# The evacuation copies of the second layer's transposed attention weights go from ScalarE to VectorE

## The chip, the cores and the metric

The kernel runs as one program on the eight cores of a Trainium2 chip. Each core takes one of the eight sequences of the batch (2048 tokens of 1024 values) through two transformer layers; the cores exchange nothing. The metric is the device time of the slowest core, in microseconds (us), from one launch. Of the engines of a core, four matter here: PE (TensorE, the matrix engine, with PEld for its weight loads), DVE (VectorE), ACT (ScalarE) and POOL (GpSimd, which issues most DMAs).

## The reference, cut to what matters

Two layers. Each normalizes x, computes attention and a mixture-of-experts feed-forward part from the normalized input, and adds both to x. Only the attention of the second layer is touched by the change:

```python
def _L1_attn_ref(x, Wq, bq, Wk, bk, Wv, bv, proj):      # 16 heads of 64
    q = jnp.einsum('bse,hde->bhsd', x, Wq) + bq[None, :, None, :]
    k = jnp.einsum('bse,hde->bhsd', x, Wk) + bk[None, :, None, :]
    v = jnp.einsum('bse,hde->bhsd', x, Wv) + bv[None, :, None, :]
    causal = jnp.triu(jnp.ones((s, s), bool), 1)
    scores = jnp.einsum('bhsd,bhtd->bhst', q, k) / scale  # scale = 8
    scores = jnp.where(causal[None, None], -jnp.inf, scores)
    att = jax.nn.softmax(scores, axis=-1) / scale
    z = jnp.einsum('bhst,bhtd->bhsd', att, v).reshape(b, s, h * dh)
    return z @ proj
```

## The kernel before, in words

The program runs stage by stage: for layer 0 the normalization with routing, the experts, q/k/v, statistics and attention, then the same for layer 1 without the statistics. Attention of layer 1 (`attn1_pass`, from line 931) is the last stage before the output is stored. x stays in SBUF all the time (`x_tm`).

`attn1_pass` walks over 16 blocks of 128 query rows (`qt` 0 to 15). Block `qt` sees `Lq = (qt+1)*128` keys because of the causal mask, so the work of a block grows from 128 to 2048 keys. This text counts blocks from 1: block 1 has 128 keys, block 16 has 2048. Inside a block the 16 heads go through a software pipeline: at step `i`, the scores of head `i` (`st_scores`), the softmax of head `i-1` (`st_soft`), and the transposes of head `i-2` (`st_pt`) are written out; after each odd head its pair's product with v (`st_ctx`) follows. A step whose transposed head is even is called an A step below (its tiles are `pbufA`, `ptbA`), the other a B step (`pbufB`, `ptbB`, then `st_ctx`).

The parts of a step, with their lines:

- Scores: PE multiplies q and k into four PSUM banks of 512 columns (`psA`, L950). DVE copies the even tiles to SBUF (`sc_sb`, L963 or L976), ACT the odd ones (L966 or L979), and DVE adds the mask to the last 128 columns (L969).
- Softmax: DVE takes the row maximum (L987) and scales it (L991), ACT computes the exponentials with their sum (L995, `pbuf`), and DVE then does three things with them: it scales the sum (L1001), takes the reciprocal (L1005), and multiplies the whole row of `pbuf` by it (L1008).
- Transposes: PE transposes `pbuf` of head `i-2` in pieces of 128 columns into PSUM (`ptp`, bf16, L1021). Each parity of head has one half of `ptp`, room for eight pieces. After eight pieces, or after the last one, they are copied to SBUF as `ptb` (L1028). In blocks 1 to 8 a head has one such copy, in blocks 9 to 16 two: the first of 1024 columns, and the second of the rest. The second group of transposes writes the same half of `ptp`, so it waits for the first copy.
- Product with v: PE multiplies v and `ptb` of both heads of the pair into `psB` (L1041); ACT copies the result out (L1051).

After each second block the output projection (L1078) is added to x (L1087).

What sets the order: every engine works through its own list in the order in which the Python code writes the operations (`Prog.op`); nothing reorders them. `flush` gives semaphores to dependencies between engines. A wait at the head of an engine's list therefore holds everything behind it on that engine, but nothing on another engine that doesn't depend on it.

Of the kernel before, what the change touches and what calls it, by code (L numbers as in the profile page):

```python
# [315 lines left out]
def build_program(T=2048, taps=(), stop_after=None):  # L316
# [19 lines left out]
    with ctx:  # L336
        p = Prog(nc, ctx)
# [593 lines left out]
        def attn1_pass(ph, q_fm, k_fm, v_tm):  # L931
# [82 lines left out]
            def st_pt(qt, h):  # L1014
                hb = h % 2
                pb = pbufA if hb == 0 else pbufB
                ptb = ptbA if hb == 0 else ptbB
                seg = []
                for kc in range(qt + 1):
                    slot = hb * 8 + kc % 8  # L1020
                    p.op("tensor", lambda e, kc=kc, slot=slot, pb=pb: e.transpose(  # L1021
                            ptp[:, slot * 128:(slot + 1) * 128],
                            pb[:, kc * 128:(kc + 1) * 128], id_b[:]),
                         r=[(pb, kc), (id_b, None)], w=[(ptp, hb)])
                    seg.append(kc)
                    if len(seg) == 8 or kc == qt:
                        k0 = seg[0]
                        p.op("scalar", lambda e, k0=k0, kc=kc, hb=hb, ptb=ptb: e.copy(  # L1028
                                ptb[:, k0 * 128:(kc + 1) * 128],
                                ptp[:, hb * 1024 + (k0 % 8) * 128:  # L1030
                                    hb * 1024 + (k0 % 8) * 128 + (kc + 1 - k0) * 128]),
                             r=[(ptp, hb)],
                             w=[(ptb, k) for k in seg])
                        seg = []
# [23 lines left out]
            for qt in range(NCH):  # L1058
                Lq = (qt + 1) * 128
                ntile = (Lq + 511) // 512  # L1060
                for i in range(16 + 3):
                    if i < 16:
                        st_scores(qt, i, Lq, ntile)
                    if 0 <= i - 1 < 16:
                        st_soft(qt, i - 1, Lq, ntile)
                    if 0 <= i - 2 < 16:
                        st_pt(qt, i - 2)
                        if (i - 2) % 2 == 1:
                            st_ctx(qt, i - 2)
# [219 lines left out]
```

How the kernel before makes its waits and increments, by code:

```python
    def wait_all_dma(self, eng, sem_name):  # L172
        s = self.dma_sems[sem_name]
        h, v = s[0], s[1]
        self.op(eng, lambda e: e.wait_ge(h, v))
# [29 lines left out]
                def body(e, entries=entries):  # L205
                    for ent in entries:
                        for (s, v) in ent.waits:
                            e.wait_ge(s, v)
                        inst = ent.fn(e)
                        for (s, k) in ent.incs:
                            inst.then_inc(s, k)
```

## Time and profile before

| | |
|---|---|
| median of 3 runs | 7202.99 us (7201.66 to 7204.07) |
| the profiled execution's own time | 7199.1 us |
| its span, core 3 (the slowest) | 7197.5 us |
| spans of the eight cores | 7181.2 to 7197.5 us |
| busy: PE / DVE / ACT | 4996.4 / 2258.2 / 1461.7 us |
| attention of layer 1, core 3 | from about 5303 to 7174 us |
| PE / DVE / ACT busy in it | 825.4 / 836.5 / 776.0 us of 1871 |

A timeline row of the profile gives the start, the duration, the engine, the line, the operation with its tiles, and in brackets how long the engine sat idle before it and what released it. Busy shares of the whole span are averages over stages with different limits: the experts' stages keep PE busy nearly all the time, while in the attention of layer 1 no engine is busy for even half of it.

### The profile page before, as it was taken

The numbers are of one execution on the slowest core, as the hardware profiler recorded it, in microseconds if no ns is written. First come the engines' busy times: TensorE is split into PE (matmuls) and PEld (weight loads), VectorE is DVE, ScalarE is ACT, GpSimd is POOL, SyncE is SP. The second block draws the span as 40 slices with busy tenths as digits, with TensorE's granted clock in tenths as the row PEclk, the third lists the DMA queues.
The fourth block names the chain that finished last, engine by engine and source line by source line (L and its number), as shares of the span: only waits on it lengthen the run. The fifth ranks groups of instructions, "written<-read, shape, count | busy, mean of one in ns | idle before, by whom it ended". The sixth has DMA issues, their size and how long they took to land. (4 is left out here: it accounts for less than half of the span.)

```text
span 7197.5 us, 67809 instructions; the slowest of 8 cores (7181.2 to 7197.5 us)
## 1 busy us (share of the span) xinstructions
PE 4996.4 (69%) x23786; PEld 2350.9 (33%) x23786; DVE 2258.2 (31%) x4515; ACT 1461.7 (20%) x2461; POOL 174.0 (2%) x318
## 2 busy tenths in 40 slices
PE   2399998673444427999999999999864444444443
PEld 2244443321111223444444444444331222222222
DVE  3333343321223232222222222222234444444443
ACT  2211110001112221101100011101013344434443
POOL 0000000000000000000000000000000000000000
PEclk9999999755666558999999999999975555555555
DMA  1122211003222102212222122220101000000001
GB/s 48 28 37 36 36 24 30 7 15 47 38 35 33 21 0 49 45 28 37 49 37 40 21 49 49 37 40 9 30 15 18 12 12 1 12 12 1 12 1 56
DMA packets 70700, 199.15 MB, mean 28 GB/s; under 512 B 8025, under 2 KB 28762, under 8 KB 60512
## 3 DMA queue, kind: packets, MB, share of 16 engines
q0 software_dynamic: 63136, 177.79, 14.9%
q1 hardware_dynamic: 7232, 17.02, 0.7%
q8 instruction: 198, 3.24, 0.2%
q14 instruction: 134, 1.10, 0.1%
HBM read 364.17 MB, written 8.39 MB: 52 GB/s over the span
## 5 line engine op out<-in xcount | busy, mean ns | idle before, releaser
L1141 PE MATMUL p_gps<-s_xn_fm,s_wgr 128*128 128x512 bf16 x4672 | 1773.4, 380 | 32.8 <-DMA s_wgr<-wg 32.8
L1149 PE MATMUL p_gps<-s_xn_fm,s_wur 128*128 128x512 bf16 x4672 | 1773.2, 380 | 12.2 <-DMA s_wur<-wu 12.2
L1167 PE MATMUL p_yps<-s_wd_sb,s_hfm 128*128 128x512 bf16 x4672 | 1011.6, 379 | 0.2 <-DVE s_x_tm L1175 0.2
L1160 DVE TENSOR_TENSOR s_hfm<-p_gps,s_sil 128x512 bf16<-128x512 f32 x584 | 403.8, 691 | 1656.4 <-ACT s_sil L1158 1656.4
L1158 ACT ACTIVATE s_sil<-p_gps 128x512 f32<-128x512 f32 x584 | 348.7, 597 | 2565.1 <-PE p_gps L1141 2508.7
L1141 PEld LDWEIGHTS p_gps<-s_xn_fm,s_wgr 128*128 128x128 bf16 x4672 | 457.6, 98 | 585.3 <-issue 35.4
L1149 PEld LDWEIGHTS p_gps<-s_xn_fm,s_wur 128*128 128x128 bf16 x4672 | 457.6, 98 | 565.8 <-issue 16.2
L1167 PEld LDWEIGHTS p_yps<-s_wd_sb,s_hfm 128*128 128x128 bf16 x4672 | 452.7, 98 | 556.0 <-issue 33.9
L1175 DVE SCALAR_TENSOR_TENSOR s_x_tm<-p_yps,s_cw_tm,s_x_tm 128x1024 f32<-128x1024 f32 x256 | 328.6, 1284 | 499.7 <-PE p_yps L1167 499.6
L1021 PE MATMUL p_ptp<-s_id_b,s_pbufB 128*128 128x128 bf16 x1088 | 147.9, 306 | 430.8 <-ACT s_ptbB L1028 271.8
L1021 PE MATMUL p_ptp<-s_id_b,s_pbufA 128*128 128x128 bf16 x1088 | 148.3, 306 | 341.3 <-ACT s_ptbA L1028 282.2
L987 DVE TENSOR_REDUCE s_sm_sc<-s_sc_sb 128x1 f32<-128x128 f32 (+15 forms) x256 | 326.5, 1276 | 0.1
L511 PE MATMUL p_xtp<-s_id_f,s_xnrot 128*128 128x128 f32 x256 | 62.1, 423 | 349.6 <-DVE s_xnrot L507 349.6
L950 PE MATMUL p_psA<-s_k_fm,s_q_fm 64*128 64x512 bf16 (+3 forms) x640 | 274.4, 554 | 22.5 <-DVE s_sc_sb L969 8.7
L918 PE MATMUL p_psA<-s_woring,s_cfm 128*128 128x512 bf16 x256 | 121.1, 585 | 233.7 <-DMA s_woring<-woT 212.9
L761 PE MATMUL p_pq<-s_xn_fm,s_wring 128*128 128x512 bf16 x1024 | 244.4, 383 | 52.3 <-DVE s_q_fm L771 19.7
L976 DVE COPY s_sc_sb<-p_psA 128x512 f32<-128x512 f32 x256 | 176.1, 690 | 303.8 <-PE p_psA L950 303.8
L1021 PEld LDWEIGHTS p_ptp<-s_id_b,s_pbufB 128*128 128x128 bf16 x1088 | 102.6, 136 | 514.6 <-issue 514.6
L1041 PE MATMUL p_psB<-s_ptbB,s_v_tm 128*64 128x128 bf16 x1088 | 138.9, 310 | 166.9 <-ACT s_ptbB L1028 166.9
L1021 PEld LDWEIGHTS p_ptp<-s_id_b,s_pbufA 128*128 128x128 bf16 x1088 | 101.6, 136 | 423.6 <-issue 423.6
L995 ACT ACTIVATE s_pbufA<-s_sc_sb,s_sm_sc 128x128 bf16<-128x128 f32 (+15 forms) x128 | 153.7, 1201 | 332.1 <-DVE s_sm_sc L991 332.1
L995 ACT ACTIVATE s_pbufB<-s_sc_sb,s_sm_sc 128x128 bf16<-128x128 f32 (+15 forms) x128 | 153.7, 1201 | 240.8 <-DVE s_sm_sc L991 240.3
(191 smaller groups left out, 4039.7 us busy)
## 6 DMA issues: line engine op xcount, KB each, us to landing
s_woring<-woT POOLq DMA_DIRECT2D x128, 256.0 KB, 4.4
s_wgr<-wg POOLq DMA_DIRECT2D x29, 1024.0 KB, 16.7
s_wur<-wu POOLq DMA_DIRECT2D x29, 1024.0 KB, 21.6
s_wd_sb<-wd POOLq DMA_DIRECT2D x10, 2816.0 KB, 20.8
s_prring<-proj POOLq DMA_DIRECT2D x64, 256.0 KB, 4.2
s_wd_sb<-wd POOLq DMA_DIRECT2D x9, 1024.0 KB, 10.0
s_x_tm<-x SPq DMA_DIRECT2D x1, 8192.0 KB, 32.0
out<-s_x_tm SPq DMA_DIRECT2D x1, 8192.0 KB, 22.5
```

Of the source, the lines that this page charges most:

```text
L761: p.op("tensor", lambda e, dc=dc, ts=ts, slot=slot, oc_l=oc_l: e.matmul(pq[:, (ts % 4) * 512:(ts % 4) * 512 + TS], wring[:, slot * 2048 + ...
L950: p.op("tensor", lambda e, oc=oc, prt=prt, qt=qt, j0=j0, w512=w512, bk=bk: e.matmul(psA[:, bk * 512:bk * 512 + w512], q_fm[prt:prt + 64, o ...
L976: e.tensor_copy(sc_sb[:, hb * T + j0:hb * T + j0 + w512], psA[:, bk * 512:bk * 512 + w512])
L987: p.op("vector", lambda e, Lq=Lq, hb=hb: e.reduce_max(sm_sc[:, hb * 4:hb * 4 + 1], sc_sb[:, hb * T:hb * T + Lq], axis=AX.X, negate=True), ...
L995: p.op("scalar", lambda e, pb=pb, Lq=Lq, hb=hb, qt=qt: e.activation(pb[:, 0:Lq], sc_sb[:, hb * T:hb * T + Lq], AF.Exp, bias=sm_sc[:, hb * ...
L1021: p.op("tensor", lambda e, kc=kc, slot=slot, pb=pb: e.transpose(ptp[:, slot * 128:(slot + 1) * 128], pb[:, kc * 128:(kc + 1) * 128], id_b[:]),
L1141: p.op("tensor", lambda e, dc=dc, ts=ts, lo=lo, rslot=rslot, gp=gp: e.matmul(gp, wgr[:, rslot * 4096 + dc * 512 + lo: rslot * 4096 + dc * ...
L1149: p.op("tensor", lambda e, dc=dc, ts=ts, lo=lo, rslot=rslot, up=up: e.matmul(up, wur[:, rslot * 4096 + dc * 512 + lo: rslot * 4096 + dc * ...
L1158: p.op("scalar", lambda e, ssl=ssl, gp=gp, gb=gb: e.activation(ssl, gp, AF.Silu), r=[(gps, ("g", gb))], w=[(sil, gb)])
L1160: p.op("vector", lambda e, fc=fc, ts=ts, ssl=ssl, up=up, gb=gb: e.tensor_tensor(hfm[:, fc * T + ts * TSL:fc * T + (ts + 1) * TSL], up, ssl ...
L1167: p.op("tensor", lambda e, fc=fc, half=half, c=c, yb=yb: e.matmul(yps[:, yb * 1024 + half * 512:yb * 1024 + (half + 1) * 512], hfm[:, fc * ...
L1175: p.op("vector", lambda e, c=c, yb=yb, e_=e_: e.scalar_tensor_tensor(x_tm[:, c * D:(c + 1) * D], yps[:, yb * 1024:(yb + 1) * 1024], cw_tm[ ...
```

## The change

One line. The copy of the transposed weights from PSUM to SBUF (L1028) is issued on the VectorE instead of the ScalarE, with the same operands; it has the same place in the code, in `st_pt`, behind the softmax of the head before.

```diff
@@ -1025,7 +1025,7 @@
                     seg.append(kc)
                     if len(seg) == 8 or kc == qt:
                         k0 = seg[0]
-                        p.op("scalar", lambda e, k0=k0, kc=kc, hb=hb, ptb=ptb: e.copy(
+                        p.op("vector", lambda e, k0=k0, kc=kc, hb=hb, ptb=ptb: e.tensor_copy(
                                 ptb[:, k0 * 128:(kc + 1) * 128],
                                 ptp[:, hb * 1024 + (k0 % 8) * 128:
                                     hb * 1024 + (k0 % 8) * 128 + (kc + 1 - k0) * 128]),
```

The lists of PE, POOL and SP stay as they are. Two places show what moves. First the DVE's list in block 4 (512 keys), before; each step is one softmax with the score copies of the next head behind it (`s_pbufA`/`s_pbufB` are the weights, `s_sc_sb` the scores, `p_psA` their PSUM banks):

```order
L1008 TENSOR_SCALAR s_pbufA<-s_pbufA,s_sm_sc 128x512
L963 COPY s_sc_sb<-p_psA 128x384
L969 TENSOR_TENSOR s_sc_sb<-p_psA,s_causal 128x128
L987 TENSOR_REDUCE s_sm_sc<-s_sc_sb 128x1
L991 TENSOR_SCALAR s_sm_sc<-s_sm_sc 128x1
L1001 TENSOR_SCALAR s_sm_sc<-s_sm_sc 128x1
L1005 RECIPROCAL s_sm_sc<-s_sm_sc 128x1
L1008 TENSOR_SCALAR s_pbufB<-s_pbufB,s_sm_sc 128x512
```

The same place on DVE after the change:

```order
L1008 TENSOR_SCALAR s_pbufA<-s_pbufA,s_sm_sc 128x512
L1028 COPY s_ptbB<-p_ptp 128x512
L963 COPY s_sc_sb<-p_psA 128x384
L969 TENSOR_TENSOR s_sc_sb<-p_psA,s_causal 128x128
L987 TENSOR_REDUCE s_sm_sc<-s_sc_sb 128x1
L991 TENSOR_SCALAR s_sm_sc<-s_sm_sc 128x1
L1001 TENSOR_SCALAR s_sm_sc<-s_sm_sc 128x1
L1005 RECIPROCAL s_sm_sc<-s_sm_sc 128x1
L1008 TENSOR_SCALAR s_pbufB<-s_pbufB,s_sm_sc 128x512
L1028 COPY s_ptbA<-p_ptp 128x512
```

The copy of the other parity's head now stands between the multiplication of L1008 and the next score copy. On ACT in block 16 (2048 keys), this stood before, with the copy behind the exponential of L995:

```order
L966 COPY s_sc_sb<-p_psA 128x384
L995 ACTIVATE s_pbufB,s_sm_sc<-s_sc_sb,s_sm_sc 128x2048
L1028 COPY s_ptbA<-p_ptp 128x1024 x2
L979 COPY s_sc_sb<-p_psA 128x512
L966 COPY s_sc_sb<-p_psA 128x384
L995 ACTIVATE s_pbufA,s_sm_sc<-s_sc_sb,s_sm_sc 128x2048
L1028 COPY s_ptbB<-p_ptp 128x1024 x2
L1051 CAST s_zfm<-p_psB 64x128 x2
```

and on DVE in block 16 this stands after the change:

```order
L987 TENSOR_REDUCE s_sm_sc<-s_sc_sb 128x1
L991 TENSOR_SCALAR s_sm_sc<-s_sm_sc 128x1
L1001 TENSOR_SCALAR s_sm_sc<-s_sm_sc 128x1
L1005 RECIPROCAL s_sm_sc<-s_sm_sc 128x1
L1008 TENSOR_SCALAR s_pbufB<-s_pbufB,s_sm_sc 128x2048
L1028 COPY s_ptbA<-p_ptp 128x1024 x2
L976 COPY s_sc_sb<-p_psA 128x512 x2
L969 TENSOR_TENSOR s_sc_sb<-p_psA,s_causal 128x128
```

Both copies of a head have gone from behind the exponential on ACT to behind L1008 on DVE.

## Rows read from the trace of the kernel before

**Rows 1.** Waits, core 3, 5303 to 7174 us: us in total, times, longest.

```profile
ACT s_pbufA L995 <- DVE s_sm_sc L991: 332.1, 127, 28.9
...
PE p_ptp L1021 <- ACT s_ptbA L1028: 282.2, 64, 5.9
PE p_ptp L1021 <- ACT s_ptbB L1028: 271.8, 64, 5.7
...
DVE s_sm_sc L1001 <- ACT s_pbufB L995: 202.0, 128, 4.1
```

**Rows 2.** Busy time by stretch: us, PE, PEld, DVE, ACT, POOL, granted clock.

```profile
5303.00:5870.00 567.00, 237.55 (x1316) 105.68 (x1315) 267.73 (x840) 213.72 (x527) 12.67 (x24) 0.51 0.08 12
5870.00:7174.00 1304.00, 587.83 (x3930) 314.34 (x3928) 568.73 (x1056) 562.29 (x847) 20.07 (x38) 0.51 0.05 8
```

**Rows 3.** Timeline, an A step of block 16: start, us, engine, line, operation.

```profile
7076.57 0.99 ACT L1028 COPY s_ptbA<-p_ptp 128x1024 bf16<-128x1024 bf16 x1
...
7077.30 0.75 DVE L1008 TENSOR_SCALAR s_pbufB<-s_pbufB,s_sm_sc 128x2048 bf16<-128x2048 bf16 x1
...
7077.70 1.01 PE L1021 MATMUL p_ptp<-s_id_b,s_pbufA 128*128 128x128 bf16 x8 [5.68 <-ACT s_ptbA L1028]
...
7078.65 1.88 PE L950 MATMUL p_psA<-s_k_fm,s_q_fm 64*128 64x512 bf16 x4
7078.81 1.01 ACT L1028 COPY s_ptbA<-p_ptp 128x1024 bf16<-128x1024 bf16 x1 [1.25 <-PE p_ptp L1021]
...
7079.71 1.29 DVE L976 COPY s_sc_sb<-p_psA 128x512 f32<-128x512 f32 x2 [1.66 <-PE p_psA L950]
```

**Rows 4.** Timeline, the B step of block 16 before it, from its second copy.

```profile
7066.20 1.01 ACT L1028 COPY s_ptbB<-p_ptp 128x1024 bf16<-128x1024 bf16 x1 [1.25 <-PE p_ptp L1021]
...
7069.17 1.88 PE L950 MATMUL p_psA<-s_k_fm,s_q_fm 64*128 64x512 bf16 x4
```

**Rows 5.** Timeline of block 4: a B step, then an A step.

```profile
5481.49 0.56 ACT L1028 COPY s_ptbB<-p_ptp 128x512 bf16<-128x512 bf16 x1
...
5482.22 0.35 DVE L1008 TENSOR_SCALAR s_pbufA<-s_pbufA,s_sm_sc 128x512 bf16<-128x512 bf16 x1
...
5482.74 0.61 PE L950 MATMUL p_psA<-s_k_fm,s_q_fm 64*128 64x512 bf16 x1
...
5483.45 0.56 DVE L963 COPY s_sc_sb<-p_psA 128x384 f32<-128x384 f32 x1 [0.88 <-PE p_psA L950]
...
5486.60 0.35 DVE L1008 TENSOR_SCALAR s_pbufB<-s_pbufB,s_sm_sc 128x512 bf16<-128x512 bf16 x1
5486.87 0.55 DVE L963 COPY s_sc_sb<-p_psA 128x384 f32<-128x384 f32 x1
```

**Rows 6.** ACT by line and shape: count | busy us, mean ns | idle before.

```profile
L1028 ACT COPY s_ptbB<-p_ptp 128x1024 bf16<-128x1024 bf16 x80 | 79.6, 996 | 14.0 <-PE p_ptp L1021 13.9
...
L1028 ACT COPY s_ptbB<-p_ptp 128x128 bf16<-128x128 bf16 x16 | 4.1, 256 | 5.2 <-PE p_ptp L1021 5.2
```

**Rows 7.** DVE by line and shape, PSUM sources: count | busy us, mean ns | idle before.

```profile
L516 DVE CAST s_xn_fm<-p_xtp 128x1024 bf16<-128x1024 f32 x32 | 39.2, 1225 | 70.1 <-PE p_xtp L511 70.1
...
L963 DVE COPY s_sc_sb<-p_psA 128x128 f32<-128x128 f32 x32 | 9.2, 289 | 3.5 <-PE p_psA L950 3.5
```

**Rows 8.** DVE by line and shape, SBUF sources.

```profile
L843 DVE TENSOR_SCALAR s_ssc<-s_ssc,s_tthr 128x512 f32<-128x512 f32 x28 | 13.6, 486 | 3.0
...
L1008 DVE TENSOR_SCALAR s_pbufB<-s_pbufB,s_sm_sc 128x1152 bf16<-128x1152 bf16 x8 | 4.2, 520 | 1.2 <-DVE s_sm_sc L1005 0.5
...
L1008 DVE TENSOR_SCALAR s_pbufB<-s_pbufB,s_sm_sc 128x1024 bf16<-128x1024 bf16 x8 | 3.9, 487 | 0.9
...
L1008 DVE TENSOR_SCALAR s_pbufB<-s_pbufB,s_sm_sc 128x128 bf16<-128x128 bf16 x8 | 2.0, 254 | 0.9
...
L843 DVE TENSOR_SCALAR s_ssc<-s_ssc,s_tthr 128x256 f32<-128x256 f32 x4 | 1.4, 353 | 0.4
```

**Rows 9.** Timeline, last B copy of block 7: no exponential stands before it.

```profile
5809.89 0.91 ACT L1028 COPY s_ptbB<-p_ptp 128x896 bf16<-128x896 bf16 x1 [1.35 <-PE p_ptp L1021]
```

## The prediction

> **What bounds the kernel now.** I read the page's busy times first, then the busy times of each stretch, then the waits, and then the timeline of single steps. The experts' stages are not touched, so only the attention of layer 1 counts, 1871 us at the end of the program. There no engine is the bound by its busy time: in the first stretch (blocks 1 to 7 and the start of block 8) DVE is busy for 268 of 567 us, in the second for 569 of 1304, and no engine has more than 47% in either [rows 2]. The granted clock is 0.51 in both, the lower of its two levels (1.2 GHz), so a slower stage has no clock left to lose. The stage is a chain of hand-overs. The waits show it: PE waits 554 us for the copies of L1028 (282.2 and 271.8), ACT waits 332 us for DVE before the exponentials of one parity, and DVE waits 202 us for the exponentials of one parity [rows 1].
>
> The timeline shows how a step closes. In an A step of block 16 the first L1028 copy starts on ACT the moment the exponential is done (7076.57) and ends at 7077.56. PE starts the second group of transposes 0.14 us later, the next scores come behind them at 7078.65, and DVE, idle for 1.66 us, starts the next score copies at 7079.71 [rows 3]. Those feed the next maximum and the next exponential. So both the exponential and the copy behind it are on the loop. In a B step PE also waits for the second copy (7066.20 to 7067.21) before the product with v, and the next scores come only behind that product, at 7069.17 [rows 4]. In block 4 a B step closes in the same way: copy at 5481.49, product, scores at 5482.74, DVE idle 0.88 us until 5483.45. An A step there has no such wait: the score copy starts at 5486.87, before L1008 has formally ended at 5486.95, so DVE itself closes the step [rows 5].
>
> **The price of the moved copy.** The change takes 384 copies off ACT (for each of 16 heads one in each of blocks 1 to 8 and two in each of blocks 9 to 16) and puts them on DVE. On ACT they cost 0.256 us for 128 columns and 0.996 for 1024 [rows 6]. A DVE copy of bf16 from PSUM stands nowhere in the trace. From above it is bounded by f32 from PSUM, 0.289 us for 128 columns and 1.225 for 1024, which is 1.045 ns per column [rows 7]. From below it is bounded by bf16 from SBUF, 0.254 and 0.487 us, 0.26 ns per column [rows 8]. In SBUF, f32 costs (486 - 353) / 256 = 0.52 ns per column [rows 8], so there 2-byte values go through at twice the rate of 4-byte ones. I take the PSUM row and halve its rate in the same way, keeping its fixed part (289 - 134 = 155 ns): 0.155 + 0.52 per 1000 columns, so 0.222 us for 128 columns, 0.69 for 1024. That is an estimate from these rows; both ends stay in the range.
>
> The Trainium skill bears on it, in "VectorE: DVE Perf Modes", section "Why PSUM operands drop a tier": a PSUM source rules out the mode that uses both read ports, but leaves the one that packs two 16-bit values per read. The table in "The TRN2 errata" of the same page would give (120 + 512) / 0.96 GHz = 0.66 us for 1024 columns, an estimate by that page, and a sum about 5 us below mine. But the same page of the Trainium skill, under "Mode 1× (REGULAR) — the baseline", names PSUM operands among the cases that the unpacked mode is there for. By that, the time would be that of the slow copy among the rivals. No row here decides between them.
>
> **What the place costs.** The expensive part is where the copy stands, not how long it takes. On ACT it starts when the exponential ends. On DVE it stands behind L1001, L1005 and L1008, all three of which wait for the same exponential. L1008 starts 0.73 us after the point where the ACT copy started, in block 4 (5482.22 - 5481.49) and in block 16 (7077.30 - 7076.57) alike [rows 3, 5]. So the copy starts later by 0.73 us plus L1008's own time, less the 0.08 us by which the next DVE instruction starts before it ends [rows 5]. L1008 lasts 0.25 us in block 1, 0.49 in block 8, 0.52 in block 9 [rows 8] and 0.75 in block 16 [rows 3].
>
> - B step, blocks 1 to 8: later by 0.73 + L1008 - 0.08, and the copy itself is shorter (0.22 for 0.26, 0.69 for 0.99). Block 1: 0.73 + 0.25 - 0.08 - 0.03 = 0.87. Block 8: 0.73 + 0.49 - 0.08 - 0.30 = 0.84. Mean 0.86, all on the loop, because PE does the product and then the next scores, for which DVE waits.
> - A step, blocks 1 to 8: DVE closes the step, so the copy is simply added to it: 0.22 - 0.08 = 0.14 up to 0.69 - 0.08 = 0.61, mean 0.38. On ACT it was hidden: nothing waited for it in such a step, as the product comes a step later.
> - A step, blocks 9 to 16: the first copy (1024 columns) ends later by 0.73 + 0.52 - 0.08 - 0.30 = 0.87 in block 9 and 1.10 in block 16, mean 0.99. The second copy is hidden: in block 16 it can start 1.25 us after the first one ended and would be done at 1.94, while the next scores are ready for DVE only at 2.15 (7079.71 - 7077.56) [rows 3].
> - B step, blocks 9 to 16: the same 0.99, less what the second copy saves (0.03 for 128 columns, 0.32 for 1024 against the 1.01 of [rows 4]), 0.17 in the mean: 0.82.
> - The last B copies of each block have no exponential ahead of them on ACT [rows 9], and on DVE L1008 had to come before the transposes anyway. They only get cheaper: by 0.17 in blocks 1 to 8, by 0.30 + 0.17 = 0.47 in blocks 9 to 16. In blocks 1 to 8 the last A copy is off the path too.
>
> A block has 8 A and 8 B steps. Blocks 1 to 8: 8 x (7 x 0.86 + 7 x 0.38 - 0.17) = 8 x 8.51 = 68. Blocks 9 to 16: 8 x (7 x 0.82 + 8 x 0.99 - 0.47) = 8 x 13.19 = 106. The sum is +174 us. ACT is relieved of 384 copies, which buys nothing: before the exponentials it waits for DVE's L991 in any case [rows 1]. The profiled execution took 7199.1 us, so the sum is 7199 + 174 = 7373; the median of the runs lies 4 us above the profiled one, which makes 7377.
>
> With the copy at its upper bound, blocks 1 to 8 gain another 0.30 per step (mean of 576 columns), and blocks 9 to 16 another 0.54 for the first copy and 0.30 for the second in B steps, in A steps some 0.1 where the second copy would now pass the ready scores (1.25 + 1.225 = 2.48 against 2.15 in block 16, none in block 9). That is 8 x (15 x 0.30) = 36 and 8 x (7 x 0.84 + 8 x 0.64 + 0.84) = 95: +305 us, 7508. With the lower bound each copy is shorter than mine by 0.20 for 1024 columns and by 0.09 in the mean of the others: 8 x 15 x 0.09 = 11 and 8 x (8 x 0.29 + 8 x 0.20) = 31 less: +132 us, 7335.
>
> **Rivals.**
> The slow copy: a bf16 copy from PSUM at the f32 rate. For it: every PSUM row that I have runs at 1.045 ns per column, the one that writes bf16 too [rows 7]. Against it: its sources are all 4-byte. 7508 us.
>
> The delay is absorbed: PE idles more than half of the stage [rows 2], so a later copy might find room and leave the time at 7203. Against it: PE's idle time is the wait for just these copies, and DVE sits idle until the scores behind them are there [rows 3, 5].
>
> The copy escapes the exponential: the copy's data, the transposes, are ready well before, and DVE idles while the exponential runs. If DVE's copy ran in that gap, PE's second transposes and the product would no longer wait for the exponential at all. Counting only the shorter copies (0.17 and 0.47 per head), that gives at least 8 x (16 x 0.17 + 16 x 0.47) = 82 us less, 7121 us. It decides by the order alone: L1028 would have to stand before L1001 on DVE. It stands behind L1008 in every step, so the chance is small.
>
> **How the numbers follow.** The forecast, 7377, has 0.80; the slow copy 0.12; absorbed 0.03; escape 0.03; the last 0.02 is for a loss beyond all of these. The likeliest one's own range is 7335 to 7430. The range for 8 in 10 takes in both bounds of the copy's price: 7330 to 7508. What a measurement of this kernel can tell from no change is about 0.2%, 14 us. Slower holds forecast and slow copy and the rest beyond, 0.94; the same 0.03, faster 0.03.
>
> **What would show it.** After the change, the L1028 rows on DVE should read 0.69 us for 1024 columns and 0.22 for 128, and start 0.08 us before L1008 ends. In block 16 the scores behind an A step start 9.48 us after those behind the B step before it now (7078.65 - 7069.17) [rows 3, 4]; that should become 10.6 us. A pair of steps in block 4 should take 1.2 us more than before. PE's waits for L1028 should name DVE and grow by about 1 us each in blocks 9 to 16. DVE's busy time should grow by about 205 us (384 copies of 0.53 us in the mean), ACT's fall by some 290 (384 of 0.75). The forecast is wrong if the copies start before L1008, if DVE's idle time before L963 and L976 in B steps shrinks by as much as the copy is late, or if the copy's rate is 1.045 ns per column.

## The result, and the profile after

The changed kernel takes 7366.3 us in the median against 7203.6 us of the kernel before, ten runs each; the ratio is 1.0224, with a 95% interval of 1.0212 to 1.0236. It is slower by 163 us. Runs disturbed by a slower state of the chip are left out of this ratio and all that follow, so single medians can differ from it. The profiled execution has a span of 7362.5 us on its slowest core, core 7, 165 us more than before.

The busy times of the page say what moved:

```profile
PE 5003.5 (68%) x23786; PEld 2352.4 (32%) x23786; DVE 2440.8 (33%) x4899; ACT 1194.4 (16%) x2077; POOL 174.0 (2%) x318
```

DVE has 384 instructions and 183 us more than before, ACT 384 fewer and 267 us less. The two engines together do less work and the kernel takes longer: the copies are cheaper on DVE. Their rows, by line and shape (count | busy us, mean ns of one), answer to [rows 6]:

```profile
L1028 DVE COPY s_ptbB<-p_ptp 128x1024 bf16<-128x1024 bf16 x80 | 54.8, 685 | 13.9 <-PE p_ptp L1021 13.9
...
L1028 DVE COPY s_ptbB<-p_ptp 128x512 bf16<-128x512 bf16 x16 | 6.7, 421 | 7.2 <-PE p_ptp L1021 7.2
...
L1028 DVE COPY s_ptbB<-p_ptp 128x128 bf16<-128x128 bf16 x16 | 3.5, 222 | 4.5 <-PE p_ptp L1021 4.5
```

The slope is (685 - 222) / 896 = 0.52 ns per column, half of the f32 rate in [rows 7].

The page's groups of PE show where the time went. Behind the second bar they give how long PE sat idle before the group, and what it waited for. They answer to [rows 1], where PE waited 282.2 and 271.8 us for these copies:

```profile
L1021 PE MATMUL p_ptp<-s_id_b,s_pbufB 128*128 128x128 bf16 x1088 | 148.2, 306 | 483.7 <-DVE s_ptbB L1028 322.9
L1021 PE MATMUL p_ptp<-s_id_b,s_pbufA 128*128 128x128 bf16 x1088 | 149.2, 307 | 402.4 <-DVE s_ptbA L1028 345.7
...
L1041 PE MATMUL p_psB<-s_ptbB,s_v_tm 128*64 128x128 bf16 x1088 | 138.9, 310 | 233.2 <-DVE s_ptbB L1028 231.1
```

PE's waits for the copies in the first two groups grew from 554 to 669 us, by 115 us in 128 waits, 0.9 us each. In the third, the product with v, PE waited 166.9 us for them before and 231.1 now.

The timeline of an A step of block 16 answers to [rows 3, 4]; its first line is where the scores of the B step before it begin (start, us, engine, line, operation, idle before). Before the change, the step of [rows 3] had this line just ahead of its first copy, ACT's read of the exponential's sum:

```profile
7076.48 0.19 ACT L995 ACTIVATION_READ_ACCUMULATOR s_pbufB<-s_sc_sb,s_sm_sc 128x1 f32 x1
```

After it:

```profile
7229.63 1.88 PE L950 MATMUL p_psA<-s_k_fm,s_q_fm 64*128 64x512 bf16 x4
7231.45 1.04 PE L1021 MATMUL p_ptp<-s_id_b,s_pbufA 128*128 128x128 bf16 x8
...
7236.94 0.19 ACT L995 ACTIVATION_READ_ACCUMULATOR s_pbufB<-s_sc_sb,s_sm_sc 128x1 f32 x1
7237.23 0.15 DVE L1001 TENSOR_SCALAR s_sm_sc<-s_sm_sc 128x1 f32<-128x1 f32 x1 [2.30 <-ACT s_pbufB L995]
7237.48 0.16 DVE L1005 RECIPROCAL s_sm_sc<-s_sm_sc 128x1 f32<-128x1 f32 x1
7237.76 0.75 DVE L1008 TENSOR_SCALAR s_pbufB<-s_pbufB,s_sm_sc 128x2048 bf16<-128x2048 bf16 x1
7238.43 0.68 DVE L1028 COPY s_ptbA<-p_ptp 128x1024 bf16<-128x1024 bf16 x1
7239.25 1.01 PE L1021 MATMUL p_ptp<-s_id_b,s_pbufA 128*128 128x128 bf16 x8 [6.77 <-DVE s_ptbA L1028]
7240.20 1.88 PE L950 MATMUL p_psA<-s_k_fm,s_q_fm 64*128 64x512 bf16 x4
7240.37 0.69 DVE L1028 COPY s_ptbA<-p_ptp 128x1024 bf16<-128x1024 bf16 x1 [1.26 <-PE p_ptp L1021]
7240.98 1.47 DVE L976 COPY s_sc_sb<-p_psA 128x512 f32<-128x512 f32 x2
```

The first copy waits for nothing but its turn: its transposes were done at 7232.49. It starts 0.08 us before L1008 ends, and 1.49 us after the read of the exponential's sum began (7236.94). On ACT it started 0.09 us after that read began, so it is late by 1.40 us, which is the 0.73 + 0.75 - 0.08 of the prediction. From scores to scores it takes 10.57 us, against 9.48 before. The second copy ends at 7241.06, 0.08 us behind the start of the score copies.

In block 4 the B step closes like this, to be set beside [rows 5]:

```profile
5497.38 0.35 DVE L1008 TENSOR_SCALAR s_pbufA<-s_pbufA,s_sm_sc 128x512 bf16<-128x512 bf16 x1
5497.65 0.42 DVE L1028 COPY s_ptbB<-p_ptp 128x512 bf16<-128x512 bf16 x1
...
5498.32 0.29 PE L1041 MATMUL p_psB<-s_ptbB,s_v_tm 128*64 128x128 bf16 x1 [3.41 <-DVE s_ptbB L1028]
...
5498.86 0.60 PE L950 MATMUL p_psA<-s_k_fm,s_q_fm 64*128 64x512 bf16 x1
...
5499.57 0.56 DVE L963 COPY s_sc_sb<-p_psA 128x384 f32<-128x384 f32 x1 [1.50 <-PE p_psA L950]
```

DVE now idles 1.50 us before its score copy, 0.88 before.

I took the length of each step as the distance between the starts of two successive row maxima (L987), and use the usual value inside a block (us):

| kernel | block 4: A, B | block 9: A, B | block 16: A, B |
|---|---|---|---|
| before | 3.41, 4.38 | 5.79, 7.44 | 9.47, 12.61 |
| changed | 3.74, 5.39 | 6.66, 8.38 | 10.56, 13.40 |

### The profile page after: what moved, and what is told of

The parts are those of the page before. It is cut to its first block and busy times, and to the rows that moved or that the text cites. A ratio compares the mean times of both kernels' runs of the same rounds, so it can differ in the third digit from the quotient of the medians.

```text
span 7362.5 us, 67794 instructions; the slowest of 8 cores (7348.5 to 7362.5 us)
## 1 busy us (share of the span) xinstructions
PE 5003.5 (68%) x23786; PEld 2352.4 (32%) x23786; DVE 2440.8 (33%) x4899; ACT 1194.4 (16%) x2077; POOL 174.0 (2%) x318
## 5 line engine op out<-in xcount | busy, mean ns | idle before, releaser
L987 DVE TENSOR_REDUCE s_sm_sc<-s_sc_sb 128x1 f32<-128x128 f32 (+15 forms) x256 | 326.6, 1276 | 0.1
L1041 PE MATMUL p_psB<-s_ptbB,s_v_tm 128*64 128x128 bf16 x1088 | 138.9, 310 | 233.2 <-DVE s_ptbB L1028 231.1
L995 ACT ACTIVATE s_pbufA<-s_sc_sb,s_sm_sc 128x128 bf16<-128x128 f32 (+15 forms) x128 | 154.0, 1203 | 380.4 <-DVE s_sm_sc L991 380.4
L1041 PEld LDWEIGHTS p_psB<-s_ptbB,s_v_tm 128*64 128x64 bf16 x1088 | 112.3, 167 | 253.4 <-issue 253.4
```

Source lines behind the costliest of these rows:

```text
L987: p.op("vector", lambda e, Lq=Lq, hb=hb: e.reduce_max(sm_sc[:, hb * 4:hb * 4 + 1], sc_sb[:, hb * T:hb * T + Lq], axis=AX.X, negate=True), ...
L995: p.op("scalar", lambda e, pb=pb, Lq=Lq, hb=hb, qt=qt: e.activation(pb[:, 0:Lq], sc_sb[:, hb * T:hb * T + Lq], AF.Exp, bias=sm_sc[:, hb * ...
L1041: p.op("tensor", lambda e, kc=kc, g=g, hh=hh, ptg=ptg, qt=qt: e.matmul(psB[(g * 64):(g * 64 + 64), g * 512:g * 512 + 128], v_tm[:, kc * D ...
```

## The experiments

Theory: the loss comes from where the copies stand in DVE's list, behind L1001, L1005 and L1008 and so behind the exponential; DVE itself is not the wrong engine. Rivals: DVE's time for them is the loss; L1008 has no part in it; the second copies carry it; a delayed A step is caught up in the B step behind it. In all kernels `st_pt` and `st_soft` compute what they did, in another order or on another engine; line numbers shift by a few where lines were added.

**Copies in DVE's gap.** `st_soft` is cut behind the exponential (L995); what followed (L1001, L1005, L1008) becomes `st_norm`. Copies on DVE as in the changed kernel.

```diff
                         st_soft(qt, i - 1, Lq, ntile)
                     if 0 <= i - 2 < 16:
                         st_pt(qt, i - 2)
-                        if (i - 2) % 2 == 1:
-                            st_ctx(qt, i - 2)
+                    if 0 <= i - 1 < 16:
+                        st_norm(qt, i - 1, Lq, ntile)
+                    if 0 <= i - 2 < 16 and (i - 2) % 2 == 1:
+                        st_ctx(qt, i - 2)
```

> The copies stay on DVE, but stand between L991 and the scaling of the sum (L1001 of before), so in the gap in which DVE waits for the exponential. My theory (the cost is the place behind L1001, L1005 and L1008, and the wait for the exponential): the copy is then free of the exponential and closes nothing. Block 16: an A step of about 7.9 us (9.47 before, 10.56 after), a B step of about 9.9 (12.61, 13.40). Block 4: an A step stays at 3.4 us, a B step falls from 4.38 to about 3.4. Sum over the blocks about 275 us less than before: 6930 us, 6870 to 7000. Rival (DVE is the wrong engine for these copies wherever they stand): slower than before, by the 205 us of copies on DVE, less what of it lies in the gap: 7250 to 7400.

Measured: ratio to before 0.961 (0.951 to 0.971), profiled 6946.8 us, 252 us less than the profiled time before, with the same 384 copies on DVE. Block 16: A 7.63, B 9.86; block 4: 3.41, 3.48. The timeline of an A step of block 16 (the copy is L1032 here, L1012 is L1008 of before):

```profile
6802.62 0.69 DVE L1032 COPY s_ptbA<-p_ptp 128x1024 bf16<-128x1024 bf16 x1
6802.76 2.00 ACT L995 ACTIVATE s_pbufB<-s_sc_sb,s_sm_sc 128x2048 bf16<-128x2048 f32 x1 [2.94 <-DVE s_sm_sc L991]
6803.45 1.01 PE L1025 MATMUL p_ptp<-s_id_b,s_pbufA 128*128 128x128 bf16 x8 [3.23 <-DVE s_ptbA L1032]
6804.40 1.89 PE L950 MATMUL p_psA<-s_k_fm,s_q_fm 64*128 64x512 bf16 x4
6804.57 0.69 DVE L1032 COPY s_ptbA<-p_ptp 128x1024 bf16<-128x1024 bf16 x1 [1.26 <-PE p_ptp L1025]
...
6805.70 0.75 DVE L1012 TENSOR_SCALAR s_pbufB<-s_pbufB,s_sm_sc 128x2048 bf16<-128x2048 bf16 x1
6806.37 1.28 DVE L976 COPY s_sc_sb<-p_psA 128x512 f32<-128x512 f32 x2
```

Both copies and the next scores start before the exponential ends at 6804.76. The rival of the wrong engine is out: the same copies on the same engine, at another place in its list, make the kernel faster than before.

**Copies early, on ACT.** The kernel before, with `st_soft` cut ahead of the exponential, so that `st_pt` comes before it; the same loop as above.

> The copies stay on ACT as before, but ahead of the exponential of the next head instead of behind it. My theory (place, not engine, decides): close to the kernel with the copies in DVE's gap. In the long blocks the exponential now waits for the second copy (some 0.7 us), in exchange the product and the next scores no longer wait for the exponential. Block 16: A and B step both about 8.5 us. Sum about 280 us less than before: 6920 us, 6860 to 7010. Rival (the engine decides, ACT is the better one in any place, or the exponential's delay eats the gain): within 50 us of before, 7150 to 7250.

Measured: 0.963 (0.954 to 0.972), profiled 6937.9 us. Block 16: A 7.94, B 8.14; block 4: 3.41, 3.41. So the place is worth 261 us on ACT. On DVE it is worth 417 us (7364.0 to 6946.8). With the copies early, the two engines are within 10 us of each other in total, but not in the steps. Inside the blocks, from the first to the last row maximum, ACT needs 47 us less (1210.7 against 1257.7), mostly in the B steps of the long blocks. The kernel on DVE makes up for most of it outside: its stage begins 9 us earlier, and the stretches behind the last row maxima are 29 us shorter. What the experiments on the loads show, further down, bears on that. Early or late, the place decides more than the engine does.

**One instruction earlier.** The changed kernel, cut ahead of L1008.

> The copies on DVE stand ahead of L1008 and behind L1005, one instruction earlier than in the changed kernel. My theory: B steps of blocks 1 to 8 gain L1008's length (0.25 to 0.49 us), A steps there nothing; in blocks 9 to 16 the first copy gains 0.52 to 0.75 us, but L1008 now waits for the second copy, which returns 0.15 to 0.45 us in A steps. Sum 79 us less than the changed kernel: 7287 us, 7260 to 7310, still slower than before. Rival (the delay is all the wait for the exponential, L1008 has no part): 7366 us.

Measured: 1.008 (1.004 to 1.012), profiled 7264.9 us, 99 us less than the changed kernel's profiled time where 79 was expected. B step of block 4: 4.96 (5.39 with L1008 in front, a gain of 0.43 for L1008's 0.35); block 16: A 9.81, B 12.57. Inside the blocks the kernel is 100 us shorter than the changed one, which had lost 183 there, so L1008 accounts for more than half of the loss. The A steps gained more than the theory had: 0.17 us in block 4 where it had nothing, and 0.75 in block 16 where it had 0.30.

**Only blocks 1 to 8.**

```diff
-                        p.op("scalar", lambda e, ...: e.copy(
+                        p.op("vector" if qt < 8 else "scalar", ...
```

The edit is against the kernel before, and the dots stand for operands that stay.

> The copies go to DVE only in blocks 1 to 8 (one copy per head), and stay on ACT in blocks 9 to 16. My theory: +68 us over before, 7271 us, 7260 to 7280; steps of blocks 9 to 16 as before. Rival (the loss sits in the second copies and their hand-over alone): 7203 us. A second question: the changed kernel's output projections (L1078 to L1087) were each about 2 us shorter than before. If that comes with the copies on DVE, it shows here in blocks 2 to 8 only.

Measured: 1.005 (1.001 to 1.010), profiled 7251.7 us. The steps are exactly those of the changed kernel in blocks 1 to 8 (block 4: 3.74, 5.39) and those of before from block 9 on (block 16: 9.48, 12.60). From the first to the last row maximum of each block, blocks 1 to 8 together grew by 70 us in it as in the changed kernel. The total grew by 53 us only. Of the 18 us between, 7.5 are that the stage began earlier (5291.7 against 5299.2), and the rest are mostly shorter output projections, in blocks 10 to 16 too, where every copy is on ACT. More on that below.

**Only the second copies** (`k0 == 8`), ACT for the rest.

> Only the second copy of a head (blocks 9 to 16) goes to DVE; the first stays on ACT behind the exponential. My theory: the second copy on DVE is hidden in A steps, as in the changed kernel, and shorter in B steps (0.03 us in block 9, 0.32 in block 16). A steps of block 16 stay at 9.47 us, B steps fall from 12.61 to about 12.3; 11 us less than before, 7192 us, 7185 to 7200. Rival (every copy on DVE lies on the path, as DVE closes the loop through its score copies): longer by up to 0.4 us a step, 7203 + 8 x 8 x 0.4 = 7229 us.

Measured: 0.998 (0.992 to 1.004); the lowest runs are 7169.0 against 7196.4 us. Block 16: A 9.47, unchanged, B 12.37 (12.61 before); block 9: 5.80, 7.48. The second copy on DVE is free in A steps, as the theory has it. In B steps it gains 0.24 us in block 16, where the theory had 0.32, and loses 0.04 in block 9, where it had a gain of 0.03. Between the two profiled executions lie 30 us (7199.1 and 7169.1). The stage beginning 11 us earlier is part of that, and the shorter projections are most of the rest. Up to the last but one row maximum of each block, the steps themselves gave 6 us, where the theory had 11.

**Only even heads** (`hb == 0`).

> Only the copies of even heads (A steps) go to DVE, those of odd heads stay on ACT. My theory: A steps lengthen as in the changed kernel (block 4: 3.41 to 3.74 us; block 16: 9.47 to 10.56), B steps stay (4.38; 12.61). Over the blocks 8 x 7 x 0.38 + 8 x 8 x 0.99 = 84 us more than before; if the shorter projections that all kernels with a copy on DVE have shown come again, less 16 us: 7271 us, 7255 to 7290. Rival (the delay of an A step is caught up in the B step behind it, since PE waits there for the copy in any case): 7203 us or less.

Measured: 1.009 (1.007 to 1.011), profiled 7265.5 us. Block 9: A 6.66, B 7.44; block 16: 10.57, 12.61. A steps lose all that they lose in the changed kernel, and nothing is caught up behind them. The B steps of blocks 1 to 5 grew as well, by 0.2 us (block 4: 4.38 to 4.58), which the theory had not, and which no run explains.

**The unchanged pair again**, on one chip.

> The kernel before, unchanged, for a second profile. The changed kernel's output projections took 21.0 us from first to last load issue against 22.9 in the kernel before, but a kernel with the copies on ACT in blocks 9 to 16 had about 21 there too. If that is a property of the kernel, this profile shows 22.9 again and the unchanged copy of the changed kernel 21.0; if it is one of the execution or chip, both are alike.

> The changed kernel, unchanged, for a second profile on the same chip as the kernel before: steps as in its first profile (block 16: A 10.56 us, B 13.40), and the projections either 21.0 us (property of the kernel) or the same as in the kernel before beside it (property of the execution).

**One single copy on DVE** (`qt == 0 and h == 1`).

> One single copy of the 384 goes to DVE, that of head 1 in block 1 (128 columns); all else is the kernel before. By its own length it is worth under 1 us. Question: in every kernel with at least some copies on DVE the loads of the output projection landed in 3.6 to 3.7 us and the eight projections were some 2 us shorter each, also in blocks whose copies were all on ACT; in the three with all copies on ACT they landed in 4.2. If that is a property of the whole program (where its data or code lies) and not of what DVE does during the stage, this kernel shows 3.6 to 3.7 us as well and takes about 7187 us; if it is tied to DVE's work in the stage, 4.2 us and 7203 us.

**The changed kernel with a long ACT list.**

```diff
+                        p.op("scalar", lambda e: e.copy(scr[:, 0:1], causal[:, 0:1]),
+                             r=[(causal, None)], w=[(scr, 0)])
```

> The changed kernel with one tiny extra copy on ACT (128x1, to a scratch tile that nothing reads) behind each of its 384 copies on DVE, so that ACT's list is as long as in the kernel before. By the steps it costs nothing: ACT is idle there, and neither the exponential nor the casts wait for it; 7366 us, 7355 to 7375. Question: what makes the projection's loads land in 3.6 to 3.7 us in kernels with many copies on DVE, and in 4.2 with none or one? If it is the length of ACT's list, this kernel lands them in 4.2 us and takes about 7382 us; if it has to do with DVE's list or the copies themselves, 3.6 to 3.7 us and 7366.

These four ask one thing, and the page's rows of the output projection's loads (KB each, median us from issue to landing) answer it. The kernel before, in its second profile:

```profile
s_prring<-proj POOLq DMA_DIRECT2D x64, 256.0 KB, 4.2
```

The changed kernel, in its second profile on the same chip:

```profile
s_prring<-proj POOLq DMA_DIRECT2D x64, 256.0 KB, 3.7
```

The times were 7201.0 and 7355.3 us. From the first to the last issue of a projection's loads, as far as the groups are complete, it took 22.7 us in this profile of the kernel before and 21.4 in that of the changed one (22.9 and 21.2 in the first profiles). One copy on DVE: 4.2, ratio 0.999 (0.996 to 1.003). The long ACT list: 3.7, profiled 7364.2 us. All eight kernels with 128 or more of the copies on DVE, and the long ACT list is one of them, landed these loads in 3.6 to 3.7 us; the two kernels with none (in three profiles) and the one with a single copy took 4.2. So the difference goes with the program and not with the execution or the chip, and the length of ACT's list is not its cause. What in the program it is, the runs leave open: the length of DVE's list, for one, was not varied by itself.

The same pages settle that it is not what DVE does in this stage. Layer 0 loads its own projection weights in pieces of 256 KB too, and its attention is over (at about 2450 us) before the first of the moved copies runs, at about 5300. The kernel before and the changed kernel, second profiles:

```profile
s_woring<-woT POOLq DMA_DIRECT2D x128, 256.0 KB, 4.3
```

```profile
s_woring<-woT POOLq DMA_DIRECT2D x128, 256.0 KB, 3.9
```

With none or one of the copies on DVE these loads took 4.2 to 4.4 us, with 128 or more 3.8 to 3.9, and 4.1 in the last kernel below.

**The version that beats both.** Copies ahead of the exponential, with `st_soft` split as in the kernel of early copies on ACT, the first of a head on ACT, the second on DVE.

```diff
-                        p.op("scalar", lambda e, ...: e.copy(
+                        p.op("vector" if k0 == 8 else "scalar", ...
```

> Copies ahead of the exponential: the first copy of a head on ACT, the second on DVE in its gap behind L991. In the kernel with both copies early on ACT the exponential waited for the second copy. My theory: that wait goes (0.7 us in block 16, little in block 9), and DVE does the second copy while it would wait for the exponential. Block 16: A and B steps about 7.3 us (7.94 and 8.14 with both on ACT); blocks 1 to 8 as with both on ACT, 3.41 us in block 4. Sum about 80 us less than with both on ACT: 6860 us, 6830 to 6900. Rival (the next step's bound is PE or the hand-over, not the exponential): no gain, 6935 us.

Measured: 0.954 (0.951 to 0.956), profiled 6863.3 us, 336 us less than before and 500 less than the changed kernel. Block 4: 3.41, 3.41; block 16: A 7.42, B 7.97. The sum came as forecast, but B steps of block 16 did not reach the 7.3 us of the theory. An A step of block 16 (copies at L1034):

```profile
6723.79 2.28 DVE L987 TENSOR_REDUCE s_sm_sc<-s_sc_sb 128x1 f32<-128x2048 f32 x1
6723.97 1.01 ACT L1034 COPY s_ptbA<-p_ptp 128x1024 bf16<-128x1024 bf16 x1 [0.49 <-PE p_ptp L1026]
6725.12 1.01 PE L1026 MATMUL p_ptp<-s_id_b,s_pbufA 128*128 128x128 bf16 x8 [1.25 <-ACT s_ptbA L1034]
...
6726.17 0.15 DVE L991 TENSOR_SCALAR s_sm_sc<-s_sm_sc 128x1 f32<-128x1 f32 x1
6726.35 0.69 DVE L1034 COPY s_ptbA<-p_ptp 128x1024 bf16<-128x1024 bf16 x1
6726.42 2.00 ACT L1000 ACTIVATE s_pbufB<-s_sc_sb,s_sm_sc 128x2048 bf16<-128x2048 f32 x1 [1.44 <-DVE s_sm_sc L991]
```

The first copy fills ACT's wait for the maximum, the second DVE's wait for the exponential, which starts 0.10 us after L991 (6726.17 + 0.15).

## Why the prediction was right

Forecast 7377, measured 7366. The mechanism was right: the copy's place in DVE's list, behind the exponential and L1008, is what costs. The sum is that close partly by luck, because two misses of opposite sign partly cancel. Step by step:

- The price of a copy was taken as 0.222 us for 128 columns and 0.69 for 1024; the rows read 0.222 and 0.685. Halving the PSUM rate for 2-byte values was right, and the rival of the slow copy (7508) fell with it.
- The measured rate agrees with the section "Why PSUM operands drop a tier" of the Trainium skill's "VectorE: DVE Perf Modes". The 0.66 us worked out from the table in that page's section "The TRN2 errata" is 4% too low here, and the unpacked mode of the Trainium skill's "Mode 1× (REGULAR) — the baseline" is not what this copy ran in. The prediction put the sum by that table 5 us below its own. Each copy would be 0.03 us shorter by it, and with as many copies as the sum counts that is about 9 us, an estimate from that page's figure.
- A steps of blocks 1 to 8: forecast +0.14 to +0.61; block 1 went from 2.12 to 2.26, block 4 by 0.33, block 8 from 4.64 to 5.24.
- A steps of blocks 9 to 16: forecast +0.87 and +1.10, measured +0.87 and +1.09. The second copy is hidden, but not by the margin forecast. The prediction read the next scores as ready for DVE 2.15 us after the first copy's end, with the second copy done at 1.94. In the changed kernel DVE begins its score copies 1.87 us after it, and the second copy ends at 1.95. That costs nothing, and with the second copies alone on DVE an A step of block 16 stays at 9.47 us.
- B steps of blocks 9 to 16: forecast +0.84 in block 9 and 0.78 in block 16 (1.10 - 0.32), measured +0.94 and +0.79.
- B steps of blocks 1 to 8: forecast +0.86, measured +0.93 to +1.03. This term was too small. Most of what is missing is a hand-over: PE began the product 0.25 us after the DVE copy (5498.07 to 5498.32), and 0.15 after the ACT copy before (5482.05 to 5482.20). It was 0.25 us in blocks 1 to 12, and 0.15 in blocks 13 to 16. Why, no run shows.
- Not forecast: the output projections got shorter, from the first to the last issue of their loads by 1.7 us (22.9 to 21.2). DVE's wait for them fell by more, from 227.4 us in eight times to 190.0, because the last copies of a block are now its own and stand behind L1008, which was its last work before: in block 16 they end 5.4 us after it (7311.63 against 7306.26).
- DVE's busy time was to grow by about 205 us and ACT's to fall by 290: 183 and 267. The copies' own rows do add up to 204 us on DVE and 289 on ACT. Busy time counts an overlap with the instruction before or behind only once, such as the 0.08 us between L1008 and the copy.
- The rival that the delay is absorbed is out by the time itself, and the kernel of even heads shows it for A steps alone: their delay comes out in full. The rival that the copies escape the exponential was wrong for this change and right as a mechanism: with the order that it asks for, the same copies on the same engine gave 252 us less than before, three times the 82 us that I counted for it. I had priced only the shorter copies and not the waits that go.

Split by place, the forecast's terms and the two spans read like this (us). "Up to the last but one row maximum" is the time from the first row maximum (L987) of a block to its fifteenth, summed over the blocks; "the end" of a block is the rest, up to the next block's first row maximum or the end of the program.

| | forecast | measured |
|---|---|---|
| blocks up to the last but one row maximum | +157.4 | +164.3 |
| ends of the 8 blocks without a projection behind them | +8.1 | +8.0 |
| ends of the 8 blocks with one | +8.1 | -5.8 |
| beginning of the stage | 0 | -1.5 |
| sum | +174 | +165 |

The steps cost 7 us more than forecast, and the ends with a projection, 14 us less. Another 2 us of the 11 are that the median lay 4 us above the profiled time before, and 2 above it after. The second pair of profiles gave +163.8, +8.0, -0.1 and -17.3, together 154: what the steps cost repeats within 0.5 us, and the projections and the beginning of the stage do not.

What stays open is why loads land faster in programs with many copies on DVE. That it shows in layer 0 already fits the beginning of the stage: its first row maximum came at 5288 to 5293 us in seven of their profiles and at 5299 to 5305 in the four with none or one. Two with many lie between, at 5295.6 (long ACT list) and 5297.7 (the changed kernel's first profile).

## What to carry to other kernels

When an operation is moved to another engine, look first at what stands ahead of it in the new engine's list and what that waits for: here copies that became 13% (128 columns) to 31% (1024) cheaper made the kernel 2.2% slower, since three instructions that come behind the same exponential stood ahead of them. Then look for the gap where the engine waits anyway, and move the operation there in the code: the same copies, placed ahead of the wait, were worth 3.9%, and 4.6% when split over both engines' gaps. The 267 us of work taken off ACT, which waited for DVE in any case, bought nothing. The distance between two successive occurrences of one instruction of the loop, read per step, gave what the steps cost to within 7 us of the forecast and 0.5 us of a second profile.

## What the runs showed of the hardware

- A VectorE copy of bf16 from PSUM to SBUF took 0.222, 0.421 and 0.685 us for 128, 512 and 1024 columns on 128 partitions; on ScalarE it was 0.256 and 0.996 us for 128 and 1024.
- TensorE began a product 0.25 us after the recorded end of the VectorE copy that it waited for in blocks 1 to 12, and 0.15 us after it in blocks 13 to 16; after a ScalarE copy it was 0.15. No run shows why.
- Loads of 256 KB landed in 3.6 to 3.7 us in some programs and in 4.2 in others that issue the same loads, on three chips and in repeated profiles. In the two pairs of profiles the ends of blocks with a projection came out 14 and 8 us below the forecast, and the stage began 1.5 and 17 us earlier. Differences of that size (0.2 to 0.3%) between two kernels here need not come from the lines that were changed.
- The granted clock of the attention stage was 0.51 before and after, the lower of its two levels (1.2 GHz), so none of the difference is the clock's.
